# A grouped convolution and a product with a sign matrix: the second double convolved by three products, signs 128 bytes further on, rows of ScalarE and VectorE in another order

## The reference

```python
out = lax.conv_general_dilated(x, weight, window_strides=(1,), padding=[(4, 4)],
                               dimension_numbers=('NCH', 'OIH', 'NCH'), feature_group_count=4)
out = out + (c @ c_weight.T)[:, :, None] + bias[None, :, None]
w = kernel.astype(x.dtype) * 2.0 - 1.0            # kernel: 1024 x 1024 bool
return x + scale * jnp.einsum('bsi,if->bsf', out, w)
```

## Time and profile before

| what | us |
|---|---|
| median of 3 runs | 171.03 |
| lowest and highest | 170.11, 171.05 |
| the profiled execution, its own time | 170.11 |
| its span, first to last instruction | 168.3 |
| TensorE busy | 162.8 (97%) |
| VectorE busy | 137.0 (81%) |
| ScalarE busy | 71.5 (42%) |
| GpSimd busy | 40.1 (24%) |

### The profile page before, as it was taken

The page is one execution under the profiler, slowest core; times in us unless marked ns, Lnnn a source line. Parts: engine busy times, 40 slices in busy tenths (PEclk is TensorE's granted clock), DMA queues, the critical chain, the costliest instruction groups (busy, mean ns, idle before and its releaser), DMA issues.

```text
span 168.3 us, 2770 instructions
## 1 busy us (share of the span) xinstructions
PE 162.8 (97%) x918; PEld 136.3 (81%) x918; DVE 137.0 (81%) x180; ACT 71.5 (42%) x65; POOL 40.1 (24%) x47
## 2 busy tenths in 40 slices
PE   7999999999999999999999999999999999999992
PEld 2469889898888779888998889887998879888782
DVE  4827567978999999779986999779977999779843
ACT  3327493570991058423772079124762071204100
POOL 5621820005130424006400433014400622000000
PEclk9999999999999999999999999999999999999999
DMA  5889489777899878697898879897988682806024
GB/s 201 252 183 321 117 230 189 181 105 186 140 344 250 255 144 314 136 245 210 214 306 206 238 143 356 182 268 132 318 219 220 102 275 64 186 0 246 7 86 164
DMA packets 27037, 33.38 MB, mean 198 GB/s; under 512 B 3536, under 2 KB 19344, under 8 KB 27024
## 3 DMA queue, kind: packets, MB, share of 16 engines
q1 hardware_dynamic: 21600, 25.36, 55.7%
q10 hardware_dynamic: 4912, 6.78, 15.0%
q0 software_dynamic: 512, 1.07, 2.8%
HBM read 10.06 MB, written 8.40 MB: 110 GB/s over the span
## 4 chain that ended last, share of the span: by engine, by line
PE 90%; DMA 4%; DVE 3%; issue 1%; ACT 1%; DVEq 0%; ACTq 0%
PE ps_A L845 30%; PE ps_conv L826 19%; PE ps_C L845 16%; PE ps_conv L801 8%; PE ps_B L845 8%; PE ps_C L861 2%; PE ps_B L861 2%; PE ps_toep L861 2%; PE ps_A L861 2%; DMA x_nat<-x 2%; DMA x_blk<-x_phase 2%; PE ps_C L787 1%; DVE x_nat L663 1%; ACT x_phase L245 1%; DVE x_nat L649 0%
## 5 line engine op out<-in xcount | busy, mean ns | idle before, releaser
L491 ACT CAST hi<-sums 128x1024 fp32r<-128x1024 f32 x14 | 14.7, 1049 | 42.1 <-DVE sums L628 30.5
L410 POOL TENSOR_TENSOR set<-x_blk 128x512 f32<-128x512 f32 x12 | 16.2, 1366 | 68.0 <-DMA x_blk<-x_phase 68.0
L649 DVE SCALAR_TENSOR_TENSOR x_nat<-ps_A,scale_col,x_nat 128x512 f32<-128x512 f32 x27 | 20.2, 749 | 13.8 <-PE ps_A L845 12.9
L448 ACT COPY x_phase<-x_nat 128x1032 f32<-128x1032 f32 x13 | 27.2, 2133 | 2.9 <-issue 2.9
L491 ACT CAST hi<-y_sum 128x1024 fp32r<-128x1024 f32 (+1 forms) x14 | 11.7, 833 | 27.8 <-DMA y_sum<-y_two 21.6
L845 PE MATMUL ps_A<-sign_T,hi 128*128 128x512 f32 x80 | 22.3, 400 | 0.0
L845 PE MATMUL ps_A<-sign_T,lo 128*128 128x512 f32 x80 | 21.8, 395 | 0.0
L845 PEld LDWEIGHTS ps_A<-sign_T,lo 128*128 128x128 f32 x80 | 15.1, 189 | 3.5
L826 PE MATMUL ps_conv<-toeplitz,w_bytes 128*128 128x128 f32 x144 | 17.2, 276 | 0.4 <-DVE y_two L602 0.4
L826 PEld LDWEIGHTS ps_conv<-toeplitz,set 128*128 128x128 f32 x144 | 16.9, 192 | 0.7 <-issue 0.2
L410 POOL TENSOR_TENSOR w_bytes<-x_blk 128x512 f32<-128x512 f32 x12 | 12.3, 1049 | 21.2 <-DVE sums L628 11.2
(11 more groups left out here) (108 smaller groups left out, 238.6 us busy)
## 6 DMA issues: line engine op xcount, KB each, us to landing
x_nat<-x SPq DMA_DIRECT2D x16, 512.0 KB, 4.4
out<-x_nat SPq DMA_DIRECT2D x15, 512.0 KB, 4.9
x_blk<-x_phase SPq DMA_DIRECT2D x114, 64.5 KB, 2.9
y_sum<-y_two ACTq DMA_DIRECT2D x48, 128.0 KB, 3.4
w_bytes<-w_bool SPq DMA_DIRECT2D x2, 512.0 KB, 5.9
x_blk<-x_phase POOLq DMA_DIRECT2D x8, 64.5 KB, 3.2
shift<-shift_dram POOLq DMA_DIRECT2D x2, 256.0 KB, 6.8
x_blk<-x_phase ACTq DMA_DIRECT2D x6, 64.5 KB, 4.8
```

Source lines behind the costliest of these rows:

```text
L410: nc.gpsimd.tensor_tensor(dif[r][:, e], x_blk[r][:, :, e:e + M:2], x_blk[r][:, :, e + 1:e + 1 + M:2][:, :, 0:K], ALU.subtract).then_inc(di ...
L448: nc.scalar.copy(x_phase[r][:, :, 0:M + 1], line(d, r, 0, PAD + L + PAD).rearrange("r (m q) -> r q m", q=B)).then_inc(phase_ok[r], B)
L491: nc.scalar.copy(parts(hi_all, k), group(k)).then_inc(hi_ok[k], 1)
L649: nc.vector.scalar_tensor_tensor(there, bank[b], scale2_col[:, :], there, ALU.mult, ALU.add).then_inc(summed[k], 1)
```

## The change

Five edits. (1) The shift is made early for 4 rows, not 8; the transposes of the taps may start after the first half of them; the second pair's plain convolution writes bank 2 first and not bank 0, with fewer waits. (2) Double 1 is convolved by `fast_conv`, too, conv(1,0) after the sixth plain product, not the fifth. (3) With this its rows go through `y_two`, four DMAs per pair and `y_sum`; SyncE loads the pairs of double 2 earlier, and VectorE instead of ScalarE sorts pair (1,1). (4) The lists of ScalarE and VectorE are reordered. T1 and T4 are made whole, S1 to S4 of double 1 move from the end of `first_double` into `step(1)`. (5) A tensor of 128 bytes per partition that nobody uses stands ahead of `w_bytes`, so that this one and all sign tables begin 128 bytes later.

```diff
-EARLY = 8
+EARLY = 4
...
-CONV_AFTER = {4: 0, 6: 1}
+
+FAST_FROM = 1, 1
+CONV_AFTER = {5: 0, 6: 1}
...
+
+        offset = sb("offset", [P, 32])
...
+        def fast(d, r):
+            return d >= FAST_FROM[r]
+
+        def earlier(d, r):
+            return max(0, d - FAST_FROM[r])
+
         def order(d, r):
 
-            return 2 * (d - 2) + r
+            return earlier(d, 0) + earlier(d, 1) + (r if fast(d, 0) else 0)
...
+        def part(d, r, i):
+
+            return ps_conv[:, (2 * r + i) % 3 if d == 0 else 1 - i]
...
+            if fast(d, r):
+                eng.wait_ge(y_in[r], 16 * 4 * (earlier(d, r) + 1))
+            else:
+                eng.wait_ge(y_ok, 12)
...
-                if d < 3:
+                if fast(d - 1, r):
+                    sp.wait_ge(dif_ok[r], 2 * earlier(d, r))
+                    sp.wait_ge(odd_ok[r], earlier(d, r))
+                else:
                     sp.wait_ge(conv_done[r], 2 * d)
-                else:
-                    sp.wait_ge(dif_ok[r], 2 * (d - 2))
-                    sp.wait_ge(odd_ok[r], d - 2)
...
+                if d == 1:
+                    store(0, 1)
                 store(d, 0)
                 if last(d):
                     store_last(d)
-                else:
+                elif d > 0:
                     store(d, 1)
...
+            load(2, 0, x_in[0])
+            load(2, 1, x_in[1])
             sp.wait_ge(conv_done[0], 2)
             sp.wait_ge(phase_ok[0], 2 * B)
             for a in range(GROUPS):
                 to_block(sp, 0, a, blk_in[0][0])
-            load(2, 0, x_in[0])
             to_blocks(1, 1)
-            load(2, 1, x_in[1])
...
-                if r == 1:
+                if r == 1 and d > 2:
                     pool.wait_ge(s_ok["S4"], d - 1)
...
+                if d == 1:
+                    for k in (("A11", "A12") if r == 0 else ("A21", "A22")):
+                        act.wait_ge(lo_0[k], 1)
+                else:
+                    act.wait_ge(lo_ok["A" if r == 0 else "A22"], d - 1)
+                    for k in (("S2", "S3", "S4") if r == 0 else ("S1", "S3")):
+                        act.wait_ge(s_ok[k], d - 1)
...
                 high_0("A12")
                 high_0("A22")
                 high_0("A11")
+                high_0("A21")
                 act.wait_ge(w_in[1], 16)
                 sign("B11")
-                to_phases(1, 1)
                 sign("B12")
-                high_0("A21")
+                odd_blocks(1, 0)
                 to_phases(2, 0)
+                odd_blocks(1, 1)
+                to_parity(1, 0)
+                to_phases(2, 1)
                 high_part("A", 1)
-                to_phases(2, 1)
+                to_parity(1, 1)
+                odd_blocks(2, 0)
                 high_part("S12", 1)
-                odd_blocks(2, 0)
...
-                LOW, HIGH = slice(0, KH // 2), slice(KH // 2, KH)
...
                 low_0("A11")
+                low_0("A21")
+                dve.wait_ge(x_first[3], 16)
+                for h in range(2):
+                    wait_blocks(dve, 0, 1, h)
+                nc.vector.tensor_copy(x_phase[1][:, :, 0:M + 1],
+                                      line(1, 1, 0, PAD + L + PAD).rearrange("r (m q) -> r q m", q=B)
+                                      ).then_inc(phase_ok[1], B)
+                dve.wait_ge(toep_ok, 2)
+                nc.vector.tensor_tensor(toeplitz[:, 2], toeplitz[:, 0], toeplitz[:, 1], ALU.add).then_inc(both_ok, 1)
                 for half in range(2):
                     dve.wait_ge(w_in[half], 16)
                 sign_sums("T3", w_bytes[:, 0:KH, BANK:L], ALU.subtract, w_bytes[:, KH:B, BANK:L])
-                dve.wait_ge(toep_ok, 2)
-                nc.vector.tensor_tensor(toeplitz[:, 2], toeplitz[:, 0], toeplitz[:, 1], ALU.add).then_inc(both_ok, 1)
...
+                fast_y(1, 0)
+                plain_sum("B")
                 dve.wait_ge(sign_ok["T2"], KH)
                 dve.wait_ge(sign_ok["B22"], KH)
-                sign_sums("T1", plain("B22", LOW), ALU.subtract, plain("T2", LOW), LOW)
-                add_shift(1, 0, 0)
-                sign_sums("T1", plain("B22", HIGH), ALU.subtract, plain("T2", HIGH), HIGH)
-                add_shift(1, 0, 1)
-                plain_sum("B")
+                sign_sums("T1", plain("B22"), ALU.subtract, plain("T2"))
+                fast_y(1, 1)
                 plain_sum("C")
                 low_part("A", 1)
-                add_shift(1, 1, 0)
-                add_shift(1, 1, 1)
-                for k in s_sum:
-                    combine(k, 1)
                 plain_sum("E")
-                low_part("S12", 1)
-
-            def last_signs(u):
-
                 dve.wait_ge(sign_ok["B21"], KH)
                 dve.wait_ge(plain_done, len(PLAIN))
-                sign_sums("T4", plain("B21", u), ALU.subtract, plain("T2", u), u)
+                sign_sums("T4", plain("B21"), ALU.subtract, plain("T2"))
...
-                sum_up("C11_P2", d)
-                sum_up("C11_P1", d)
-                if runs(d, 2):
-                    fast_y(d + 1, 0)
+                    sum_up("C11_P2", d)
+                    sum_up("C11_P1", d)
+                    if runs(d, 2):
+                        fast_y(d + 1, 0)
+                else:
+                    fast_y(2, 0, ("mid", "even"))
+                    combine("S1", 1)
+                    combine("S2", 1)
+                    fast_y(2, 0, ("odd",))
+                    low_part("S12", 1)
+                    combine("S3", 1)
+                    combine("S4", 1)
+                    sum_up("C11_P2", 1)
+                    sum_up("C11_P1", 1)
...
-                if d == 1:
-                    last_signs(slice(0, KH // 2))
...
-                    if d == 1:
-                        last_signs(slice(KH // 2, KH))
...
-            pe.wait_ge(exp_ok, 2)
+            pe.wait_ge(exp_ok, 1)
             for s in range(2):
                 for u in range(B):
+                    if (s, u) == (0, B // 2):
+                        pe.wait_ge(exp_ok, 2)
...
-                    if r == 1 or d > 0:
-                        pe.wait_ge(y_ok, 8 * d + 4 * r + 2 * h - 2)
+                    if (d, r, h) == (0, 1, 1):
+                        pe.wait_ge(y_ok, 2)
...
-                    pe.wait_ge(y_ok, 16)
+                    pe.wait_ge(y_ok, 8)
...
-                        pe.wait_ge(odd_ok[r], d - 1)
+                        pe.wait_ge(odd_ok[r], earlier(d, r) + 1)
                     else:
-                        pe.wait_ge(dif_ok[r], 2 * (d - 2) + (1 if m == 0 else 2))
+                        pe.wait_ge(dif_ok[r], 2 * earlier(d, r) + (1 if m == 0 else 2))
...
-                        conv(1, CONV_AFTER[n])
+                        fast_conv(1, CONV_AFTER[n])
```

More of the change, by code:

```diff
@@ L397, in differences @@
             def differences(d, r):
-                if d > 2:
+                if earlier(d, r):
                     pool.wait_ge(m_done[0], order(d - 1, r) + 1)
@@ L411, in differences @@
                                             ALU.subtract).then_inc(dif_ok[r], 1)
-            for d in range(2, DOUBLES):
+            for d in range(1, DOUBLES):
                 for r in range(2):
-                    differences(d, r)
+                    if fast(d, r):
+                        differences(d, r)
         @block.scalar
@@ L462, in to_parity @@
             def to_parity(d, r):
-                act.wait_ge(lo_ok["A" if r == 0 else "A22"], d - 1)
-                for k in (("S2", "S3", "S4") if r == 0 else ("S1", "S3")):
-                    act.wait_ge(s_ok[k], d - 1)
+                if d == 1:
[5 more added lines that the diff above has]
+                        act.wait_ge(s_ok[k], d - 1)
                 for p, made in ((0, y_even_ok), (1, y_odd_ok)):
@@ L573, in add_shift @@
                 dve.wait_ge(conv_done[r], 2 * d + i + 1)
-                if i == 0:
+                if i == 0 and d == 0:
                     dve.wait_ge(early_ok, 1)
@@ L617, in combine @@
                 if k in ("S1", "S3"):
-                    if d == 1:
-                        dve.wait_ge(y_ok, 16)
-                    else:
-                        for r in range(2):
-                            dve.wait_ge(y_in[r], 16 * 4 * (d - 1))
+                    for r in range(2):
+                        wait_y(dve, d, r)
                 if d > 1:
@@ L800, in conv @@
                         for s in range(2):
-                            now = nc.tensor.matmul(ps_conv[:, h, g].rearrange("m u o -> m (u o)"),
+                            now = nc.tensor.matmul(part(d, r, h)[:, g].rearrange("m u o -> m (u o)"),
                                                    x_blk[r][:, 2 * g + h, s:s + M],
```

38 lines of the change are left out of this document (19 added, 19 removed).

## The result

The changed kernel takes 177.07 us, the median of 4 runs (175.64 to 177.74); the kernel before, run beside it, 170.72 (170.11 to 171.05). The ratio is 1.037, 95% interval 1.033 to 1.041: slower, by 6.4 us. The forecast was 176.9 in a range of 169.5 to 179.5. Where TensorE stands still for long, single executions of the same kernel differ in their mean granted clock and so in their time; the four here have 0.97, 0.98, 0.98 and 0.97. The profiled execution took 177.74, with a span of 175.7 and a mean clock of 0.97.

The account below looks back on a forecast made before the run. TensorE, busy 97% of the span, was taken as the bound. +4.8 us at conv(2,1), -0.25 and +1.8 for the clock made +6.4 on 170.11, 176.5; half of 0.9 added gave 176.9, range 169.5 to 179.5.

Parts of the forecast that it names:

- The beginning (-0.9): Up to the first product: narrower early shift, third bank and earlier transposes together save 0.9 us; start at 17.0, not 17.93.
- The pair by three products (-1.6): Second double's two convolutions: 24 matmuls instead of 32 each, 2.68 us instead of 3.49, so 1.6 us less TensorE work.
- The start of conv(2,0), T: Start of pair (2,0)'s convolution, forecast at 41.7: 43.77 less 0.9 and 1.6, plus 0.4.
- lower part 0.4 after it is due: Second double's first product: VectorE's lower part, queued behind conv(1,1)'s rows and a sum, ready at 38.9, 0.4 us late.
- The hole: Before conv(2,1): TensorE idle from T+2.7 to T+10.2, waiting for ScalarE's odd-block copy behind the upper part of S3 and S4.
- The clock: After TensorE stands 7.5 us: half clock for a while, costing 1.8 us, between bounds of 0 and 1.85.
- rival 1: The hole before conv(2,1) comes but the clock stays: 174.7 to 175 us; chance 0.15.
- The signs (0): Sign tables moved by 128 bytes: no effect on the 512-column matmuls, 0 us, within bounds of 9 us either way.
- Rival 3: The sign table's place sets the matmul pace: 4 to 9 us off the run, 168 to 173 with the hole; chance 0.15.
- The hole at 55 us (-0.25): TensorE's small hole at 55 us goes, as the second half of T4 leaves the step: 0.25 us less.
- three signs of being wrong: S1 to S4 ready before 44, conv(2,1) within 2 us of conv(2,0), or a steady double not 18.4 us.
- Rival 2: No hole before conv(2,1), because S4 is ready at about T+1: 166.8 us, faster; chance 0.16.

Follow-up runs that it names:

- the filled hole: The changed kernel with 36 bf16 matmuls of zeros between conv(2,0) and conv(2,1), so TensorE does not stand idle there: 174.17 us, ratio 1.021.

## Why the prediction was right, and where it was off

- **The beginning (-0.9): right as a sum.** The first product starts at 17.04; forecast 17.0. Of the terms, the smaller shift gave 0.42 and not 0.52 (11.48 to 12.11, against 11.60 to 12.65), the third bank 0.35 as reckoned (12.11 to 17.04, against 12.65 to 17.93), and the first convolution began 0.17 sooner (8.61) and not 0.05; in the run with one pair and the same split transposes it began later than before, at 9.29, so that last term isn't shown to be the change's.
- **The pair by three products (-1.6): right.** conv(1,0) started at 28.01 (forecast 28.3, at the old pace) and the next product 2.59 later, against 3.49: 1.8 us for two pairs.
- **The start of conv(2,0), T: 42.44 instead of 41.7.** The step "lower part 0.4 after it is due" was too small: the first product, due at 37.03, stood until 37.58 for the upper part, which was to hold by 0.3, and VectorE's lower part took 1.99 us instead of 1.22, beside GpSimd's two differences for (2,0), which took 3.04 us in the same stretch. With the second half started at 39.60 this cost 1.8 us instead of 0.4; the better pace (0.4 us over the 80 matmuls up to there) and the shorter convolutions (0.2) gave part of it back.
- **The hole: the mechanism was right, row by row.** conv(2,1) came 10.9 us after T (forecast 10.2). The step that was too small is again a duration: S1 and S2 took 1.35 us each, not 0.93, with GpSimd's differences for (2,1) running at 44.87 for 2.50 us. The run with the odd blocks first shows that ScalarE's row held conv(2,1): it started 7.0 us sooner. It doesn't show that the 7 us could be had, since 2.6 of them came back at once as the next hole.
- **The clock: 2.9 us in the profiled execution instead of 1.8, and 1.4 in the trace without the 128 bytes.** That it would fall was a choice between two bounds, and the filled hole shows the choice right: no lower clock, and 177.07 less 174.17. The upper bound of 1.85 was wrong, since the stretch behind the hole at 0.50 was 6 us long (53.33 to 59.36), longer than at the start of the trace. The lower bound rested on the clock column, which says 1.00 after the last matmul; it says 1.00 for 1.19 to 4.58 as well, where matmuls of 512 columns started 0.43 us apart, so at the ends of a trace it was weak evidence for rival 1. The Trainium skill ("TensorE: Matmul & The Clock Gate", The HAM clock gate) has an idle TensorE put back to half clock; after 8 us the trace agrees, and at 2.6 us idle, in the run with the odd blocks first, it stayed at 1.00 in the profile.
- **The signs (0): wrong.** "The nearest row being the same matmul on seven different tables, all at the same pace" was a poor row: all seven tables lie at multiples of 8 KB from each other, so it couldn't show a dependence on place within 256 bytes. They are worth 1.2 us in this kernel (178.26 less 177.07). Rival 3 had the place as the cause, but 4 to 9 us for it.
- **The hole at 55 us (-0.25): right.** From the second half of P6 to the third double's first product, nine half products, the kernel before took 8.72 us (50.78 to 59.50), 0.35 more than nine times 0.93; the changed kernel took 8.16 (59.87 to 68.03), nine times 0.907. The hole is gone.
- **The total** was 0.2 us off because errors cancel: T 0.7, the hole 0.7 and the clock 1.1 too small make 8.9 us instead of 6.4 up to the third double, of which the pace behind T and the hole at 55 us gave back about 0.4; then 0.9 less from there on, by the pace; and the profiled run was itself 0.7 above the median. That the total came within 0.2 us is luck; its direction and its cause are not.
- **The prediction's own signs.** The hole, what ends it and the lower clock came as said. P2 of the third double came at 68.03 and not at 65 to 66. And one of its three signs of being wrong came true: a steady double is 18.07 or 18.55 us and not 18.4, because of the pace of the products, not of the hole.
- **Rival 2** (no hole) would have had 166.8. Its condition, S4 ready at T+1, was nowhere near: S4 ended at T+9.1.

## What to carry to other kernels

An in-order engine's row matters more than its busy share: ScalarE was 40% busy, and one copy of 0.65 us behind a cast that waits for another engine held TensorE for 8 us. When a transform saves work but sends its result by DMA, count from the transfer's landing to every reader in each engine's row, before taking the saving; here 1.8 us of TensorE's work were saved and 8 lost. When a wait is removed, look for the next reader at once (three runs here moved the wait on), and where a long wait must stay, matmuls of zeros can keep the clock: 2.9 us between two traces here.

## What the hardware showed that was not expected

- The pace of a 512-column fp32r matmul depends on the places of both operands: 227 ns where they begin at the same offset within 256 bytes, 232 where they are 128 bytes apart (five placings above). Why isn't shown. The Trainium skill ("TensorE: Matmul & The Clock Gate", Back-to-back issue gap) would have 216; the traces differ, with 227 or 232.
- Some of VectorE's operations whose operands both lie in SBUF took longer while GpSimd worked: in the changed kernel S3 and S4 took 0.68 us each, and S1 and S2, which ran beside GpSimd's differences, 1.35; the lower part took 1.99 instead of 1.22. Those that read PSUM didn't: in the same trace the middle rows took 0.68 and the sums from bank A 0.75 beside GpSimd as without it. Not every one is hit, since in the run with the odd blocks first S2 took 0.69 beside GpSimd; and no run moved GpSimd's work, so this is read from what ran together, not tested.
- A standstill of 8.2 us was followed by 6.0 us at half clock and one of 7.5 us (without the 128 bytes) by 2.8; one of 3 us once by 3.7 us, and one of 2.6 us by none. Each is a single trace. The filled hole had 1.00 throughout.
